# A decoder block on one core: k, v and the gate of r stay in PSUM, half-array matmuls are issued in pairs, and the work of every engine stands in another order

## What is computed

```python
# RWKV time mix (layer_norm before it, time_shift = the token before)
k, v = xk @ Wk.T, xv @ Wv.T
sr = sigmoid(xr @ Wr.T)
rwkv = sr * wkv(time_decay, time_first, k, v)      # a scan over the tokens:
#   ww = u + kt; qq = max(pp, ww); e1 = exp(pp - qq); e2 = exp(ww - qq)
#   y = (e1 * aa + e2 * vt) / (e1 * bb + e2)
#   qq2 = max(pp + w, kt); e1b = exp(pp + w - qq2); e2b = exp(kt - qq2)
#   aa, bb, pp = e1b * aa + e2b * vt, e1b * bb + e2b, qq2
x = x + rwkv @ Wo.T
# RWKV channel mix (layer_norm, time_shift)
x = x + sigmoid(xr @ Wrec.T) * (square(relu(xk @ Wkey.T)) @ Wval.T)
# attention: for each token, 16 heads x 16 heads, causal over the heads
scores = einsum('bsqd,bskd->bsqk', q, ctx) / 4     # q = layernorm(x)
x = x + einsum('bsqk,bskd->bsqd', softmax(mask(scores)), ctx)
# feed-forward of rank 64
x = x + gelu((layernorm(x) @ U1) @ V1 + b1) @ U2 @ V2 + b2
```

## Time and profile before

| | us |
|---|---|
| median of 3 runs | 1357.65 |
| lowest and highest | 1354.46, 1358.54 |
| the profiled execution, its own time | 1354.16 |
| its span in the profile | 1352.4 |
| ScalarE's first `att_now` to its last (16 groups) | 29.59 to 1096.92 |
| from there to the end of the span | 255.5 |
| mean granted clock of TensorE | 0.92 |

### The profile page before, as it was taken

The page is one execution under the profiler, slowest core; times in us unless marked ns, Lnnn a source line. Parts: engine busy times, 40 slices in busy tenths (PEclk is TensorE's granted clock), DMA queues, the critical chain, the costliest instruction groups (busy, mean ns, idle before and its releaser), DMA issues.

```text
span 1352.4 us, 14723 instructions
## 1 busy us (share of the span) xinstructions
PE 1090.1 (81%) x3584; PEld 610.2 (45%) x3584; DVE 1076.3 (80%) x2108; ACT 1063.3 (79%) x2134; POOL 982.2 (73%) x847
## 2 busy tenths in 40 slices
PE   0479587979899897979899897979899897959626
PEld 0136354544546363544546363544536363535302
DVE  1454898898989799797989798897989798876681
ACT  8878778888888878888888878888888878566435
POOL 0211896969696988968696978968696978877580
PEclk9889789999999899999999899999999899969667
DMA  5010010001010100101010100101010100110000
GB/s 171 16 38 10 16 32 16 31 17 47 16 47 1 62 0 16 47 16 47 16 47 2 61 0 16 47 16 47 16 47 7 41 1 16 32 32 16 0 16 16
DMA packets 38961, 38.39 MB, mean 28 GB/s; under 512 B 2930, under 2 KB 38644, under 8 KB 38900
## 3 DMA queue, kind: packets, MB, share of 16 engines
q1 hardware_dynamic: 38900, 37.77, 8.7%
HBM read 29.38 MB, written 8.39 MB: 28 GB/s over the span
## 4 chain that ended last, share of the span: by engine, by line
PE 40%; DVE 23%; ACT 18%; POOL 10%; issue 7%; DMA 1%; ACTq 0%; DVEq 0%; POOLq 0%; SPq 0%
PE bank L844 16%; PE bank L920 5%; POOL prod L337 5%; PE bank L926 5%; DVE o_att L1367 5%; PE bank L851 4%; ACT n L470 4%; POOL prod L349 4%; DVE stat L1178 4%; PE bank L912 3%; PE bank L897 2%; PE bank L936 2%; PE bank L930 2%; PE bank L858 1%; DVE num L1289 1%
## 5 line engine op out<-in xcount | busy, mean ns | idle before, releaser
L349 POOL TENSOR_TENSOR prod<-prob,v_dh 128x256 f32<-128x256 f32 (+3 forms) x256 | 404.7, 1617 | 41.4 <-ACT prob L587 23.5
L337 POOL TENSOR_TENSOR prod<-q,kv_ctx 128x256 f32<-128x256 f32 (+5 forms) x448 | 405.6, 944 | 32.9 <-ACT q L470 32.9
L844 PE MATMUL bank<-xk,w_key 128*128 128x512 f32 x512 | 238.4, 614 | 20.2 <-DVE xk L1220 14.2
L1335 DVE TENSOR_REDUCE score<-prod 128x16 f32<-128x256 f32 (+5 forms) x448 | 177.2, 466 | 76.6 <-POOL prod L337 76.6
L897 PE MATMUL bank<-w_val,hidden 128*128 128x256 f32 x1024 | 229.4, 380 | 0.0
L359 POOL TENSOR_TENSOR num<-kT,vT 128x512 f32<-128x512 f32 x32 | 46.6, 1455 | 240.3 <-PE bank L851 181.5
L897 PEld LDWEIGHTS bank<-w_val,hidden 128*128 128x128 f32 x1024 | 193.4, 191 | 31.7 <-issue 7.1
L1367 DVE TENSOR_REDUCE o_att<-prod 128x64 f32<-128x256 f32 (+3 forms) x256 | 189.5, 801 | 10.0 <-POOL prod L349 10.0
L844 PEld LDWEIGHTS bank<-xk,w_key 128*128 128x128 f32 x512 | 98.7, 197 | 142.4 <-issue 117.3
L858 PE MATMUL bank<-ident,n 128*128 128x128 f32 x384 | 63.2, 311 | 123.6 <-ACT n L470 123.6
L858 PEld LDWEIGHTS bank<-ident,n 128*128 128x128 f32 x384 | 51.6, 160 | 150.0 <-issue 147.2
(11 more groups left out here) (104 smaller groups left out, 2159.4 us busy)
## 6 DMA issues: line engine op xcount, KB each, us to landing
x_in<-in_x SPq DMA_DIRECT2D x16, 512.0 KB, 4.9
kv_ctx<-in_ctx SPq DMA_DIRECT2D x16, 512.0 KB, 3.8
n<-in_x SPq DMA_DIRECT2D x16, 512.0 KB, 3.5
out<-y_out SPq DMA_DIRECT2D x16, 512.0 KB, 4.5
w_key<-in_wkey SPq DMA_DIRECT2D x1, 1024.0 KB
w_val<-in_wval SPq DMA_DIRECT2D x1, 1024.0 KB
w_k<-in_wk SPq DMA_DIRECT2D x1, 256.0 KB, 2.7
w_v<-in_wv SPq DMA_DIRECT2D x1, 256.0 KB, 2.9
```

The costliest lines, as they stand in the source:

```text
L337: ins = pool.tensor_tensor(o, a, b, ALU.mult)
L349: ins = pool.tensor_tensor(o, ph[:, HB * n:HB * n + HB, 0:keys].unsqueeze(2).to_broadcast(shape), vh[:, :, 0:keys].unsqueeze(1).to_broadca ...
L844: mm = pe.matmul(to[:, :], w[:, fi, P * f:P * f + P], src[:, fi, :], start=(fi == 0), stop=(fi == CH - 1))
L1335: ins = dve.tensor_reduce(o, src, AX.X, ALU.add)
```

## The change

1. `copy_k` and `copy_v` are gone, with their semaphores. `scan_pp` and `rise` read k in banks 0 and 1, the weighings read v in banks 2 and 3; the banks are held that long. `gate_of_r` writes tanh in place, in PSUM, and `gate_num` reads it there. `e2` has a tile of its own.
2. `weigh_token` and `weigh_bonus` go from GpSimd, which does not read PSUM here, to VectorE.
3. `project_v1`, `project_u2` and `open_with_b2` each issue two matmuls on two halves of the array (rows or columns 0 to 63 and 64 to 127) next to each other. The row of b2 and the ones are laid out at partitions 0 and 64 for it, with two more small DMAs at the start.
4. The calls in `step` of PE, DVE, ACT and POOL stand in another order; SP's order stays. ScalarE has four table loads a step, not six. GpSimd makes the first two score products of a group at the end of its step and not at the start of the next.

```diff
-            def copy_k(g, f):
-                act.wait_ge(k_mm, upto(g, 2, f + 1))
...
-                act.activation(kT[:, f, :], bank[f][:, :], ACT.Copy).then_inc(k_out, 1)
...
-                act.activation(vT[:, f, :], bank[2 + f][:, :], ACT.Copy).then_inc(v_out, 1)
...
-                act.activation(gate_r[:, f, :], bank[f][:, :], ACT.Tanh, scale=0.5).then_inc(r_gate, 1)
+                act.activation(bank[f][:, :], bank[f][:, :], ACT.Tanh, scale=0.5).then_inc(r_gate, 1)
...
             def scan_pp(g, f):
-                dve.wait_ge(k_out, upto(g, 2, f + 1))
+                dve.wait_ge(k_mm, upto(g, 2, f + 1))
...
-                                                 kT[:, f, T * s:T * s + T], START, ALU.add, ALU.max)
+                                                 bank[f][:, T * s:T * s + T], START, ALU.add, ALU.max)
...
+            def weigh_token(g, f):
+                dve.wait_ge(e2_exp, upto(g, 2, f + 1))
+                dve.wait_ge(v_mm, upto(g, 2, f + 1))
...
+                dve.tensor_tensor(num[:, f, :], e2[:, f, :], bank[V_BANK + f][:, :], ALU.mult).then_inc(e2v_done, 1)
+
+            def weigh_bonus(g, f):
+                dve.wait_ge(rr_exp, upto(g, 2, f + 1))
+                dve.wait_ge(aa_done, upto(g, 2, f + 1))
+                dve.tensor_tensor(num[:, f, :], rr[:, f, :], bank[V_BANK + f][:, :], ALU.mult).then_inc(rv_done, 1)
...
+            def project_u2(g, jj):
+                pe.wait_ge(gelu_done, upto(g, 8, 2 * jj + 2))
+                for j in (2 * jj, 2 * jj + 1):
+                    r = RANK * (j % 2)
+                    pe.matmul(bank[4][r:r + RANK, :], w_u2[:, j, :], hidden[:, j, :],
+                              start=(j < 2), stop=(j >= FT - 2)).then_inc(down_mm, 1)
...
                 if on(4):
                     if on(1):
-                        pe.wait_ge(v_out, upto(i - 1, 2))
+                        pe.wait_ge(rv_done, upto(i - 1, 2))
...
                     project_u1(i - 4)
...
                     if on(1):
-                        pe.wait_ge(r_gate, upto(i - 1, 2, 1))
+                        pe.wait_ge(gnum_done, upto(i - 1, 2, 1))
```

More of the change, by code:

```diff
@@ L263, in _ @@
                 sp.dma_start(w_v2[half, :], v2).then_inc(rest_w_loaded, 16)
-            for e in range(2):
-                sp.dma_start(b2_row[:, e, :], b2).then_inc(rest_w_loaded, 16)
+            for r in (0, RANK):
+                for e in range(2):
+                    sp.dma_start(b2_row[r:r + 1, e, :], b2).then_inc(rest_w_loaded, 16)
             def load_x(g):
@@ L656, in step @@
                     normalise_4(i - 4)
+                act.preload_act_table_set(GELU_SET)
+                if on(1):
+                    gate_of_r(i - 1, 0)
+                if on(4):
+                    copy_n4T(i - 4, 0)
+                    copy_n4T(i - 4, 1)
                 if on(2):
@@ L701, in step @@
                     gelu(i - 4, 3)
-                if on(0):
-                    shift_of(1, i)
+                if on(2):
+                    ffn_now(i - 2, 1)
                 if on(4):
@@ L772, in step @@
                     relu(i - 2, 3)
+                if on(4):
+                    copy_qT(i - 4)
+                if on(0):
+                    normalise_1(i, p)
+                if on(1):
+                    ln_den(i - 1, 1)
                 if on(2):
@@ L1491, in step @@
                     first_residual(i - 1, 1 - p, 1)
+                if on(0):
+                    att_before_r(i, 1)
+                if on(1):
+                    stats_2(i - 1, 0)
+                    stats_2(i - 1, 1)
+                    mean_2(i - 1)
+                if on(3):
+                    stats_4(i - 3, 0)
+                if on(0):
+                    weigh_token(i, 0)
+                if on(3):
+                    stats_4(i - 3, 1)
+                if on(0):
+                    weigh_token(i, 1)
+                if on(-1):
+                    mean_1(i + 1)
                 if on(3):
@@ L1494, in step @@
                 if on(0):
-                    att_before_r(i, 1)
+                    scan_aa(i, 0)
+                    weigh_bonus(i, 0)
             drive(dve, step)
```

476 lines of the change are left out of this document (204 added, 272 removed).

## The result

The changed kernel takes 1295.2 us (median of 4 runs, 1294.9 to 1296.4), the kernel before 1356.6 on the same chip: ratio 0.952, 95% interval 0.948 to 0.955. Forecast were 1284 and a range of 1254 to 1332: direction and range hold, the point is 11 us low. The profiled execution took 1296.4 us, its span 1294.5.

A forecast was written before the change was run, and what follows sets the result against it. No engine full; a loop through all engines sets the step: second half bound by TensorE, first by VectorE's and ScalarE's queue order. Steady −40, fill −20, drain −11: −71 from 1354.2, 1283, plus 1: 1284 us; range 1254 to 1332.

The forecast's parts named there:

- The walk: Loop through all engines in a steady step, summed from row durations: first key 5.5 us earlier, clean step 69.5 us.
- the four small corrections: Behind the first key: 22.9 us, +1.0 (u2), −1.0 (b2), +0.45 (a transpose), +0.3 (rec gates on ScalarE) = 23.7.
- gaps that a walk loses (0 to 2): Added to each clean step of 69.5 us for gaps missed in summing rows: 1.0 us, bounds 0 to 2.
- The clock term: TensorE's lower clock at u1 and v1, with its pause ahead of u1 kept: 1.6 us a step, bounds 0 and 3.8.
- Rival (a): u1 held by the second weigh_bonus if scan pairs ahead take 3.17 us: +3.6 a step, 1330 us; chance 0.13.
- Fill and drain: Up to 264.32: −20 us (−8 to −26), 3 of it at the start; after 1096.92: −11 (0 to −16).
- Rival (d): VectorE held by GpSimd at shift_scores (two SBUF inputs): 7.4 us a step, 1387 us; 0.09 slower, 0.05 about the same.
- Part 1: ScalarE loses four k/v copies and two table loads a step, 4.9 us; worth nothing off the end-setting path, 3 at start.

The follow-up runs named there:

- the fillers: The changed kernel plus five matmuls a step on TensorE whose result nobody reads, ahead of the transposes of norms 2 and 4: 1274.8 us, ratio 0.940.

## Why the prediction was right, and where it was off

**The walk.** In the clean step its times stand: second `gate_values` t = 13.3 (said 13.5), mean of norm 3 begun at 15.6 and done at 15.9 (16.0), GpSimd's start on q 19.8 (19.8), VectorE's string to its end 28.9 (29), n4T 35.4 (35.6), `v1` 39.4 (39.5), end of the second `gate_num` 40.4 (40.3), first `key` 45.9 (45.8), from there to the next start 24.1 (23.7), step 70.0 (69.5). Scans of k take 1.23 to 1.26 a pair, weighings 0.67 to 0.69, `b2` as a pair 1.13 (1.06 to the next row). GpSimd stands idle 12.3 us before q, against some 10. All this was worked out from rows of the other order, and where an engine's string has no wait in it, such a sum is as good as its rows. One term came out by luck: for t = 13.5 instead of 16.9 the walk names 1.7, 0.6 and a transpose (0.45), 2.8 us of the 3.4 that it takes off.

**The steady steps: 72.9, not 72.1.** Two terms were short. The clean step is 70.0 and not 69.5, nearly all of it behind the first `key` (24.1, said 23.7), where no run shows which of the four small corrections was off: 5.5 us in eleven steps. On top of it I had put 1.6 for the clock and 1.0 for gaps, 2.6; measured are 2.9, another 3 us: 19.0 us in the four steps with a turn (74.8 each) and 12.7 in the other seven (71.8 each). The size was nearly right and the mechanism not: what the prediction had as "gaps that a walk loses (0 to 2)" is no haze but mostly the turn of a loop at one known place, 2.5 to 2.8 us every second step, and I had not asked where the branch lands in the new order, though the order shows it. In the kernel before it showed no idle time, so no row warned of it; removed, it gave 15 us. The clock term was the right size by luck (the fillers took 1.7 off the mean step): not so much the engine's pause ahead of `u1` decides, as I took it, but the work before that, and in the changed kernel it hits `u1` in nearly every step and `v1` in few.

**Rival (a)** is what happened in six of ten steps: `u1` waits for the second `weigh_bonus`. I had given it 0.4 us of room and a price in stretched scans. Both occurred (the first `aa` pair took 3.2 us in five of the ten steps, else 1.35), and the turn, which I had not seen, came on top in four of the six. Its price of 3.6 a step was paid in part: the latenesses pass through one wait.

**Fill and drain.** The fill gave 12.7 us, not 20. The start gave 3.1, as said. But I took 3 to 6 for each of four steps, and the first two have not yet the strings that the new order shortens: 2.1 longer (34.0 against 31.9), 2.5 shorter, then 4.7 and 4.5. The drain gave 14.3, not 11. Together 27.0 where 31 was said, so the rest of the miss, 9 of 13 us in the span, is the steady steps (30.8 instead of 40).

**Rival (d)**, VectorE held by GpSimd, did not come: no `prob` row over 2.3 us in steady steps, one of 8.12 in the drain. The runs show why it was a fair rival, and that the change protects one of the two operations in question.

**Part 1** was undersold. "Off the end-setting path it is worth nothing" was the right question, but taken back in the new order the four copies cost 46 us and the loads 33, against some 37 and 41 that 16 steps of them take on ScalarE. The loads stand on the path for the most part; the 46 hold the stretched weighings and the turn as well. What each part gives depends on the others, and the single losses, 46 + 33 + 56 and 63 for the weighing (measured on top of the copies), add to 198 us, three times what the whole change brought.

## What to carry to other kernels

Where the order of a queue is changed, look in the new trace for idle time without a releaser where its loop's branch lands, and if there is some, move the branch: the same instructions in the same order were 12 us apart by that alone (9 by the ratios). Look at what a matmul at the lower clock had before it, and not only at its wait: a few idle matmuls in earlier pauses can be worth more than the pauses. And keep an operand in PSUM when the other engine on VectorE's port is busy: it cost nothing per operation here (0.67 to 0.69 us) and took the operation out of the phase lottery, provided that the engine that must free the bank does so early in its queue.
